# One transfer per turn and the head masks moved on GpSimd in the heads stage of a graph attention, attention and experts kernel

## The reference

```python
attn_out = _mha(x, in_proj_w, in_proj_b, out_proj_w, out_proj_b)   # 16 heads of 8 features
x = _layernorm(x + attn_out, ln1_g, ln1_b)
moe_out = _hier_moe(x, w_group, b_group, w_expert, b_expert, w1, b1, w2, b2)
x = _layernorm(x + moe_out, ln2_g, ln2_b)
```

## Time and profile before

| | before |
|---|---|
| median of 3 runs (lowest to highest) | 565.12 us (563.15 to 565.46) |
| profiled execution, its own time | 566.35 us |
| its span | 564.5 us |
| PE busy | 493.2 us (87%), granted clock 0.969 |
| DVE busy | 425.3 us (75%) |
| ACT busy | 375.2 us (66%) |
| POOL busy | 290.9 us (52%) |
| L1626, row maxima, 64 operations | 75.3 us |
| L2143, exponentials, 96 | 64.1 us |
| L717, scatter, 32 | 33.4 us |
| L725 and L732, masks, 28 and 14 | 28.5 and 14.5 us |

### The profile page before, as it was taken

The page is one execution under the profiler, slowest core; times in us unless marked ns, Lnnn a source line. Parts: engine busy times, 40 slices in busy tenths (PEclk is TensorE's granted clock), DMA queues, the critical chain, the costliest instruction groups (busy, mean ns, idle before and its releaser), DMA issues. The chain is left out here.

```text
span 564.5 us, 14903 instructions
## 1 busy us (share of the span) xinstructions
PE 493.2 (87%) x4887; PEld 330.2 (58%) x4887; DVE 425.3 (75%) x1188; ACT 375.2 (66%) x1144; POOL 290.9 (52%) x515
## 2 busy tenths in 40 slices
PE   5998899999999999999789999988987777688781
PEld 3665566667767777765345565554554455566660
DVE  3589988888888888998466788777778768656562
ACT  3557688888888877778456677656656546467550
POOL 0587653222222222045344568877686446746564
PEclk9999999999999999999999999999999988979876
DMA  8700999999999000403100000101141053243300
GB/s 348 292 3 1 283 274 272 281 276 274 282 274 269 27 0 12 138 1 150 37 3 3 1 3 21 50 20 50 40 169 49 31 140 91 80 120 108 103 30 8
DMA packets 49865, 65.13 MB, mean 115 GB/s; under 512 B 2536, under 2 KB 45557, under 8 KB 48646
## 3 DMA queue, kind: packets, MB, share of 16 engines
q1 hardware_dynamic: 47014, 57.91, 36.8%
q0 software_dynamic: 2784, 6.37, 3.2%
HBM read 20.53 MB, written 44.20 MB: 115 GB/s over the span
## 5 line engine op out<-in xcount | busy, mean ns | idle before, releaser
L1626 DVE TENSOR_REDUCE nm<-SC 128x8 f32<-128x1024 f32 x64 | 75.3, 1219 | 28.3 <-PE SC L1119 27.8
L2143 ACT ACTIVATE room_p<-ST 128x512 f32<-128x512 f32 (+1 forms) x96 | 64.1, 740 | 47.1 <-PE ST L1138 44.7
L1522 DVE TENSOR_REDUCE room_w<-SC 128x512 f32<-128x2048 f32 x32 | 73.0, 2281 | 1.0 <-PE SC L948 1.0
L615 POOL TENSOR_TENSOR spread<-parts,units 128x48 bf16<-128x48 bf16 x32 | 8.8, 276 | 122.2 <-DVE parts L1497 122.2
L2050 ACT ACTIVATE room_w<-room_w,shift 128x128 f32<-128x128 f32 x128 | 49.7, 390 | 19.0 <-DVE shift L1531 18.9
L815 POOL DMA_INDIRECT out<-room_v,id_r x39 | 38.9, 997 | 26.2 <-DVE room_v L1964 16.6
L2041 ACT ACTIVATE room_w<-ST,cv 128x128 f32<-128x128 f32 x128 | 36.4, 366 | 18.5 <-PE ST L963 18.4
L963 PEld LDWEIGHTS ST<-room_w 128*128 128x128 f32 x256 | 33.1, 191 | 15.3 <-issue 13.0
L2059 ACT ACTIVATE room_w<-room_w,inv 128x128 f32<-128x128 f32 x128 | 41.0, 407 | 0.1
L1158 PE MATMUL SC<-room_p,room_w 128*32 128x128 f32 x1024 | 36.3, 280 | 5.3 <-DVE room_w L1650 2.0
L717 POOL DMA_INDIRECT sorted_rows<-room_w,slot_i x32 | 33.4, 1044 | 13.6 <-issue 11.2
(11 more groups left out here) (306 smaller groups left out, 1344.5 us busy)
## 6 DMA issues: line engine op xcount, KB each, us to landing
sorted_rows<-w SPq DMA_DIRECT2D x8, 4290.0 KB, 41.1
room_v<-sorted_rows SPq DMA_DIRECT2D x39, 130.0 KB, 2.0
x_t<-xT SPq DMA_DIRECT2D x2, 1024.0 KB, 8.2
ctx_t<-adj SPq DMA_DIRECT2D x1, 2048.0 KB, 17.0
biased_rows<-room_w SPq DMA_DIRECT2D x2, 1024.0 KB, 4.5
room_w<-biased_rows SPq DMA_DIRECT2D x8, 256.0 KB, 3.3
room_w<-mask SPq DMA_DIRECT2D x1, 1536.0 KB
w<-weights SPq DMA_DIRECT2D x1, 1356.0 KB, 8.9
```

The lines of the kernel that those rows point to most:

```text
L1522: dve.tensor_reduce(logit[:, :, :], SC[:, :, :].rearrange("p b (i m) -> p b m i", i=TYPES), AX_X, ALU.max)\
L1626: dve.tensor_reduce(nm[:, v % 2, 2 * PER_R * pair:2 * PER_R * (pair + 1)], SC[:, 2 * pair:2 * pair + 2, :].rearrange("p r (i n) -> p (r i) ...
L2143: act.activation(ex[:, v % 2, first:last, :], ST[:, first:last, :], ACT.Exp)\
```

## The change

Four things change, nearly all on GpSimd.

1. In turns 12 to 27 the transfer (`scatter`) stands at the turn's start, right behind the wait for the turn's score products, instead of at the end of the turn before it. From turn 12 on that wait is for both halves of the scores, where it was for the first. For group 4 the transfers are at the end of turn 27, the starts of turns 28 and 29, and the end of turn 29. Group 5 stays in turn 30.
2. `mask_keys` makes the masked keys of one batch (four heads, 128 columns each, in one instruction with 4x128 elements) instead of one head of four batches. It stands behind the head parts in every turn, not ahead of them in b = 0 and b = 1. The query masks, which stood ahead of the head parts in b = 1 and b = 3, stand both behind them in b = 1.
3. `rows_x1` is cut in two: `rows_scaled` in b = 2 ahead of the head parts, `rows_moved` in b = 3 behind them, with the `row_id`.
4. TensorE waits for the masked keys of each batch (`keys_of`) instead of once a group.

```diff
+        def keys_of(v):
+
+            return PER_R if v < GB else PER_R + v - GB + 1
...
-            def rows_x1(p):
+            def rows_scaled(p):
 
                 pool.wait_ge(S("xn_ready"), p + 1)
+                pool.tensor_tensor(x1_g[:, :, :], xn[:, :, :], R("ln1g").unsqueeze(1).broadcast_to([128, GB, D]),
+                                   ALU.mult).then_inc(S("x1g_ready"), 1)
+
+            def rows_moved(p):
+
                 bc = lambda n: R(n).unsqueeze(1).broadcast_to([128, GB, D])
-                pool.tensor_tensor(x1_g[:, :, :], xn[:, :, :], bc("ln1g"), ALU.mult).then_inc(S("x1g_ready"), 1)
                 pool.wait_ge(S("x1g_ready"), p + 1)
                 pool.wait_ge(S(f"in_rows{p % 2}"), 16 * (p // 2 + 1))
                 pool.tensor_tensor(rows[:, p % 2, :, 0:D], x1_g[:, :, :], bc("ln1b"), ALU.add).then_inc(S("row_x1"), 1)
...
-            def mask_keys(g, heads):
-
+            def mask_keys(g, b):
+
+                cols = slice(b * N, (b + 1) * N)
                 pool.wait_ge(S("key_ready"), g + 1)
-                for i in heads:
-                    pool.tensor_tensor(k_m[:, g % 2, i, :], k_s[:, g % 2, :],
-                                       C("hmask")[:, i:i + 1].broadcast_to([128, GT]), ALU.mult)\
-                        .then_inc(S("km_ready"), 1)
+                pool.tensor_tensor(k_m[:, g % 2, :, cols],
+                                   k_s[:, g % 2, cols].unsqueeze(1).broadcast_to([128, PER_R, N]),
+                                   C("hmask").unsqueeze(2).broadcast_to([128, PER_R, N]), ALU.mult)\
+                    .then_inc(S("km_ready"), 1)
...
                 if batch(u + LEAD):
-                    pool.wait_ge(S("s_mm"), 2 * (u + LEAD) + 1)
-                if b == 0 and more and nxt > 0:
-                    mask_keys(nxt, (0, 1))
+                    pool.wait_ge(S("s_mm"), 2 * (u + LEAD) + (2 if u >= GB * 3 else 1))
+                if GB * 3 <= u < B - GB:
+                    scatter(norm - 1, b)
+                elif B - GB <= u < B - 2:
+                    scatter(norm - 1, b + 1)
                 if b == 0 and normed and norm < G - 2:
                     norm1_power(norm)
-                if b == 1 and more and nxt > 0:
-                    mask_keys(nxt, (2, 3))
-                    mask_queries(nxt, 0)
                 if b == 2 and normed:
-                    rows_x1(norm)
-                if b == 3 and more and nxt > 0:
-                    mask_queries(nxt, 1)
-                if normed and (u == B - 2 or b == 3 and u < B - 2):
-                    row_id(norm, 0)
+                    rows_scaled(norm)
                 if batch(u + LEAD):
                     top_parts(u + LEAD)
+                if normed and (u == B - 2 or b == 3 and u < B - 2):
+                    rows_moved(norm)
+                    row_id(norm, 0)
+                if more and nxt > 0:
+                    mask_keys(nxt, b)
+                if b == 1 and more and nxt > 0:
+                    mask_queries(nxt, 0)
+                    mask_queries(nxt, 1)
                 if u == B - 2:
                     for n in range(GB):
                         if n == GB // 2:
                             norm1_power(G - 2)
                         scatter(norm, n)
-                elif b == 3 and normed and u < B - 2:
+                if u == B - GB - 1:
                     scatter(norm, 0)
-                if b < GB - 1 and GB * 3 <= u < B - 2:
-                    scatter(norm - 1, b + 1)
                 if u == B - 3:
                     scatter(norm - 1, 3)
...
-                    pe.wait_ge(S("km_ready"), PER_R * (g + 1))
+                pe.wait_ge(S("km_ready"), keys_of(v))
```

More of the change, by code:

```diff
@@ L789, in rest @@
                     norm1_power(G - 1)
-                    rows_x1(G - 2)
+                    rows_scaled(G - 2)
+                    rows_moved(G - 2)
                 if k == 2:
```

## The result

| | before | after |
|---|---|---|
| median (lowest to highest), 9 runs each | 565.12 us (562.25 to 567.61) | 570.55 us (568.32 to 572.67) |
| ratio to before, 95% interval | | 1.0082 (1.0058 to 1.0106) |
| profiled execution, its span | 566.35, 564.5 us | 568.32, 566.5 us |
| VectorE busy | 425.3 us (75%) | 445.9 us (79%) |
| turns 8 to 11 | 21.66 us | 24.79 us |

A forecast was written before the change was run, and what follows sets the result against it. Took the bound as TensorE, nearly always busy, plus product ends signalled about 1 us late under transfers. Late signals -8.8, turns 28 to 30 -1.2, mask collisions +12.9: +2.9 on 565.12 gives 568.0 us, range 555 to 573.5.

The forecast's parts named there:

- The holds: Turns 12 to 27: exponentials start about 1 us late under a transfer; moving it gains 9.23 less 0.4, -8.8 us.
- 14 turns of 14: Kernel before: all 14 turns with late exponentials have the transfer over the picks; used as evidence against C.
- The transfer's new place costs nothing: Turns 12 to 27: behind the score products a late signal delays nobody; otherwise 1 us per turn, 16 in all.
- some 21.2 us: GpSimd's expected work sum per group after the change, under the expected group length of 24 us.
- The mask stops one link each: Turns 8 to 27: each GpSimd mask blocks one short VectorE operation; 2.5 us a group, 2.9 in turns 8 to 11, +12.9.
- Turns 28 to 30: Three late starts of 0.9 us go, moved transfers cost 1.5: -1.2 us, bounds -2.7 and +1.5.
- need the reduces' end at +2.36, so nobody waits: Turns 12 to 27: head parts need reduces ended, 2.36 us after their start; the transfer ends earlier, about +1.5 to +1.8.
- Turns 0 to 7, 0: These turns have masks but no routing chain on VectorE, so the change costs 0 there.
- The tile stage only shifts: The tile stage moves in time, with no gain or loss assigned to it.
- A: Rival, faster, chance 0.25: late starts go but mask collisions bind little; 555 us, or 558 to 562 with some collisions.
- B: Rival, slower, chance 0.13: the new mask form costs 1.27 us, each collision 0.23 longer, +3.8 in all; 571.8 us.
- C: Rival, slower, chance 0.12: the delay moves to another product or doesn't hang on place; half stays, 4.4 to 5; 572.7 us.

The follow-up runs named there:

- The fills: Kernel before with the 16 GpSimd transfers of turns 11 to 26 replaced by scratch-buffer fills: 535.63 us (0.9993) on one chip, 558.16 us (0.9829) on another.
- the repeat: The changed kernel run once more, on another chip, against the kernel before there: 572.50 us, 1.0067.

## Why the prediction was right, and where not

The forecast was 568.0, 2.9 us slower; the medians are 5.4 us apart, the heads stage of the two traces (to the exponentials of turn 31) 4.7. That it came so near is partly luck: turns 8 to 27 were put at +4.1 us and came to +2.0, turns 28 to 30 were put at -1.2 and came to +1.8, and 0.8 us came up ahead of turn 8. Step by step:

- **The holds, -8.8 us.** Right. The fills give 9.0 in the same turns, and the changed kernel has none in turns 12 to 27: its exponentials start 0.48 to 0.52 us behind the start of the picks in all of them but turn 15 (0.80, as before). The count of "14 turns of 14" was too even: in turns 19 and 23 of before the transfer ends with the picks and holds 0.3 to 0.4 us, the other nine of turns 16 to 26 about 1.0.
- **The transfer's new place costs nothing.** Right: with masks as fills, the groups are 21.66. That chip shows no holds anywhere; on the other chips it is the changed kernel's starts of the exponentials, 0.5 us behind the picks' start, that say it. GpSimd's sum of "some 21.2 us" a group was wrong without effect: its own had 17.7 to 19.5, and the changed kernel has 18.1 to 18.5.
- **The mask stops one link each.** Right in kind. In turns 8 to 11 the forecast was +2.9 and the trace has +3.13. In turns 12 to 27 it was 2.5 a group; 94.75 us for the four groups against 87.15 with fills for masks is 1.9 a group. Between the starts of the reduces the two kernels differ by 0.3 to 0.6 us a turn for b = 0 (0.5 forecast; one link, L1727, takes 0.88 instead of 0.17), by 1.31 for b = 1 (1.65) and by 0 to 0.24 for b = 2 (0.35). So b = 1 and b = 2 were put too high. Collisions came to +10.7 us in all, where the sum had 12.9.
- **GpSimd runs on into the scale in turn 10.** Not in the prediction. L702 starts right behind the three masks when no transfer stands ahead of it, and a fourth link takes 1.16 us beside it. This 1.0 us is why turns 8 to 11 seem well forecast; without it they would have come to some 2.1, by the same shortfall as the later groups. The drop of the clock, 1.2 us more in the repeat, was not in the prediction either.
- **Turns 28 to 30, -1.2 us, bounds -2.7 and +1.5.** Wrong: +1.8, outside the bounds. I counted holds and looked past the rest: VectorE's chain of counts at the end of turn 27 is stopped by L710 and a mask, the reduce starts 3.33 us behind the turn's start where it was 1.83, and TensorE idles 2.28 us instead of 0.78. That is 1.5 of the 1.7 us that turn 28 loses. The drop of the clock behind it is no mark of the change: turn 28 took 7.36 us in a trace of the kernel before without the drop and 7.70 and 7.67 in two with it, and 6.65 and 8.23 in two of the version with everything ahead of the head parts. Of the three holds that I let go, that of turn 30 stays: its exponentials start 1.72 us behind the picks' start.
- **The head parts "need the reduces' end at +2.36, so nobody waits".** True, but I took their place ahead of the masks as given and priced their lateness nowhere. They have a turn of slack, which is the reason why the best order puts them last.
- **Turns 0 to 7, 0.** Turns 0 to 3 took 20.98 and 21.73 us in the first two traces. The 0.7 us are lost in turn 0, at a granted clock of 0.71 where before had 1.00. The same kernel, the one with the head parts last, gave 21.71 with the drop on one chip and 20.99 without it on another, so the program alone does not decide it. But seven of the nine traces with moved operations have it and none of the five with the old order, so that the change has no part in it is not shown.
- **The tile stage only shifts.** Not settled. It is 2.7 us shorter in the changed kernel's first trace and 2.9 us in its repeat (105.8 against 108.6), but the three traces of the kernel before alone differ by 2.0.
- **Rivals.** A fell: the links do not slip ahead of the masks. B fell: 1045 ns. C, that the hold moves to another product, fell in turns 12 to 27; its second half, that a hold need not hang on the program alone, proved true of chips.

A reading mask stops a link of two SBUF operands until it ends, and a fill, which reads nothing, does not: 0.99 us for L1745 beside a mask, 0.19 for the same link (L1756) beside a fill. The Trainium skill ("SBUF — State Buffer", section "Who interferes with whom") says that such a link contends with a GpSimd instruction that reads SBUF and not with one that only writes; the traces agree. (Links of one operand are another matter, as the last section of this document shows.) It also says that TensorE and ScalarE never wait on anyone. It says so of SBUF's ports, and no run here tests that; read wider, it does not hold. ScalarE starts 1.95 us behind the start of TensorE's picks under a transfer on one chip and 0.66 on another, and there the measurement decides.

## What to carry to other kernels

Before an operation of GpSimd with two SBUF operands is moved, look at what VectorE runs at the new place: beside the reduces from PSUM it was free (1.22 us each in every place), beside a chain of short links each one cost up to its full length, however few elements the link had. Find the real deadline of every operation in a queue before ordering it: here the four of the head parts, which looked urgent, could go last, and that alone turned a loss of 0.7 to 0.8% into a gain of 1.1 to 1.3%. Keep GpSimd's transfers away from the end of a product that another engine waits for, and compare kernels on one chip only.

## What was unexpected of the hardware

- A transfer issued by GpSimd over the end of a product delays the waiting engine, mostly to 0.30 to 0.46 us behind the transfer's end, on the chips of the second and third set and in the first traces of before and after; on the chip of the first set it does not (at most 0.26 us behind the picks' end, inside the transfer). A fill of 1.38 us at the same place does not.
- A cast to int32 of four elements (L1758) is stopped beside a mask as well: 0.73 us in turn 14 where the free one takes 0.17, though it has one operand. The Trainium skill (the same page and section) lists casts among the operations that can take both ports; the trace agrees. Fills stop such operations of one operand too, though they read nothing: the cast L1769 took 1.15 us beside one, and L1672 took 0.80 to 1.03 beside each of the four that it met in the third set's run with fills. So a fill is not a neutral filler of GpSimd's time.
- Two masks in a row can stop one link past the end of the first, to the end of the second: 1.35 and 1.38 us. In other places the link got in between them (L1743, 0.96 us).
